# Layer 3 attention on one core: one product for q and k of a head, their parts doubled across the partitions by transfers

## What is computed

```
scale = Dh ** (-0.5)
q = (x @ Wq).reshape(B, N, H, Dh).transpose(0, 2, 1, 3)
kv = x @ Wkv
k = kv[..., :H * Dh].reshape(B, N, H, Dh).transpose(0, 2, 1, 3)
v = kv[..., H * Dh:].reshape(B, N, H, Dh).transpose(0, 2, 1, 3)
s = jnp.einsum('bhid,bhjd->bhij', q * scale, k)
gm = jax.lax.stop_gradient(jnp.max(s, axis=-1, keepdims=True))
causal_mask = jnp.triu(jnp.ones((N, N), bool), 1)
p = jnp.where(causal_mask, 0.0, jnp.exp(s - gm))
num = jnp.einsum('bhij,bhjd->bhid', p, v)
out = num / (jnp.sum(p, axis=-1, keepdims=True) + EPS)
```

## Time and profile before

| | |
|---|---|
| runs | 2026.16, 2018.31, 2021.64 us; median 2021.64 us |
| profiled execution | 2017.0 us, of it 2015.2 us from the first to the last instruction |
| busy share of that span | PE 85%, PEld 55%, DVE 71%, ACT 60%, POOL 55% |
| granted TensorE clock | 0.939 of full speed over the span |
| layer 3 attention | about 1008 to 2007 us, half of the span |

### The profile page before, as it was taken

One profiled execution on the slowest core, in us unless ns is written; L12 is line 12 of the kernel. 1 busy time (PEld: TensorE's weight loads), 2 busy tenths in 40 slices (PEclk: granted clock), 3 DMA queues, 4 the chain that ended last, 5 costly groups with the idle time before them and its releaser, 6 DMA issues. The chain is left out here.

```text
span 2015.2 us, 30793 instructions
## 1 busy us (share of the span) xinstructions
PE 1719.5 (85%) x10655; PEld 1111.6 (55%) x10655; DVE 1420.8 (71%) x2090; ACT 1200.7 (60%) x2046; POOL 1118.3 (55%) x1024
## 2 busy tenths in 40 slices
PE   6737999999577788877789999889999999989988
PEld 3414777788543377634634555555555555555564
DVE  3556777774254799854168888888888888888883
ACT  4374333326236577435358777777877777777860
POOL 1244554541400375212037888788888888888881
PEclk8667999998588999988989999999999999999999
DMA  2102222220100000004117999999889999999992
GB/s 70 35 30 76 79 85 69 84 80 26 32 6 14 13 1 1 1 11 125 43 27 136 159 159 159 163 160 162 160 154 157 159 163 166 160 159 162 164 164 58
DMA packets 632550, 193.08 MB, mean 96 GB/s; under 512 B 591601, under 2 KB 624130, under 8 KB 632398
## 3 DMA queue, kind: packets, MB, share of 16 engines
q1 hardware_dynamic: 624006, 167.56, 46.1%
q0 software_dynamic: 8224, 23.51, 3.9%
q10 hardware_dynamic: 168, 0.06, 0.0%
HBM read 36.90 MB, written 12.48 MB: 25 GB/s over the span
## 5 line engine op out<-in xcount | busy, mean ns | idle before, releaser
L2884 DVE TENSOR_REDUCE half_max<-scores 128x1 f32<-128x1024 f32 x512 | 614.8, 1219 | 131.9 <-PE scores L2666 126.3
L2583 POOL TENSOR_TENSOR p_low<-p,p_high 128x2048 f16<-128x2048 f32 (+15 forms) x256 | 576.3, 2251 | 150.7 <-ACT p_high L2810 126.0
L2666 PE MATMUL scores<-k_high,q_pair 128*128 128x512 f16 x1024 | 303.7, 378 | 66.0 <-ACT p L2795 61.1
L2795 ACT ACTIVATE p<-scores,exp_bias 128x1024 f32<-128x1024 f32 (+7 forms) x384 | 317.4, 861 | 68.5 <-DVE exp_bias L2889 66.3
L2810 ACT ACTIVATE p_high<-p 128x2048 f16<-128x2048 f32 (+15 forms) x256 | 282.6, 1104 | 40.6 <-DMA pT_high<-p_high 32.8
L2666 PE MATMUL scores<-k_low,q_pair 128*128 128x512 f16 x1024 | 304.2, 379 | 0.0
L2686 PEld LDWEIGHTS scores<-v_pair,pT_high 128*128 128x128 f16 x2176 | 149.8, 98 | 103.5 <-issue 61.4
L2686 PE MATMUL scores<-v_pair,pT_low 128*128 128x129 f16 x2176 | 183.9, 220 | 11.5 <-DMA pT_low<-p_low 11.2
L2686 PE MATMUL scores<-v_pair,pT_high 128*128 128x129 f16 x2176 | 186.4, 220 | 3.8 <-DMA pT_high<-p_high 3.6
L2686 PEld LDWEIGHTS scores<-v_pair,pT_low 128*128 128x128 f16 x2176 | 145.2, 98 | 46.7 <-DMA pT_low<-p_low 15.7
L2666 PEld LDWEIGHTS scores<-k_low,q_pair 128*128 128x128 f16 x1024 | 99.2, 97 | 121.7
(11 more groups left out here) (491 smaller groups left out, 3210.1 us busy)
## 6 DMA issues: line engine op xcount, KB each, us to landing
pT_high<-p_high SPq DMA_TRANSPOSE x256, 3.6
pT_low<-p_low SPq DMA_TRANSPOSE x256, 3.7
slots<-zero_row SPq DMA_DIRECT2D x1, 3036.0 KB, 14.1
slot_rows<-slots SPq DMA_DIRECT2D x23, 132.0 KB, 2.4
slots_out<-expert_out SPq DMA_DIRECT2D x23, 128.0 KB, 1.8
w_up<-in_L_ffn_inter_w_dram SPq DMA_DIRECT2D x1, 2048.0 KB, 8.8
x_tokens<-in_L_attn_x_dram SPq DMA_DIRECT2D x4, 256.0 KB, 3.5
dispatched<-moe_rows SPq DMA_DIRECT2D x1, 1024.0 KB, 10.3
```

The costliest lines, as they stand in the source:

```text
L2583: pool.tensor_tensor(flat(pl[:, buf, b0:b0 + n, :]), flat(p32[:, buf, b0:b0 + n, :]), flat(ph[:, buf, b0:b0 + n, :]), ALU.subtract).then_i ...
L2666: mm = pe.matmul(ps[:, b.start + i, :], q, k[:, par, cs(2 * half + i)], start=start, stop=not start)
L2795: act.activation(flat(p32[:, buf, b0 + first:b0 + first + w, :]), flat(ps[:, banks(p, half), :])[:, 0:w * P], ACT.Exp, bias=bias[:, p:p + ...
L2884: dve.tensor_reduce(mx[:, p % 2, half:half + 1], flat(ps[:, b[half], :]), AX.X, ALU.max, negate=True)\
```

## The change

q and k of a head come from one product: the tile `w_qk` holds the 64 columns of Wq and, beside them, the 64 columns of Wk of the head, so that partitions 0 to 63 of the result are q and 64 to 127 are k. A head has 4 units, not 8, in steps 0 to 3. ACT makes the high part of both with one operation, whose scale is a column (0.125 for q, 1.0 for k), DVE the low part of both. What the doubled weights did is done by eight transfers for each head, each of 64 partitions by 1024 16-bit numbers (128 KB): `move_k` writes k low and k high into the two halves of `k_pair`, and `move_q`, which waits for that, overwrites the k halves with q, so that one tile holds (q high; q low) and the other (q low; q high). SP issues them in positions 4 and 8 (`move_k`) and 6 and 10 (`move_q`), half of the tokens at a time. The loads of weights are two per head, not four, and stand in position 12, not 5. The scores take the two q tiles with the one k tile. In the prologue the moves of head 0 run one behind the other.

```diff
-                        for dst, src in ((wq, inp["L3_attn_Wq"]), (wk, inp["L3_attn_Wkv"])):
-                            for r in range(2):
-                                sp.dma_start(dst[:, h % 2, r, :], src[:, ds(h * DH, DH)]).then_inc((w_loaded0, w_loaded1)[h % 2], 16)
+                        for r, src in enumerate((inp["L3_attn_Wq"], inp["L3_attn_Wkv"])):
+                            sp.dma_start(wqk[:, h % 2, r, :], src[:, ds(h * DH, DH)]).then_inc((w_loaded0, w_loaded1)[h % 2], 16)
+                    def move_k(at, par, x):
+                        wait(sp, qk_low, at(NCH, 2 * x + 2, 1))
+                        sp.dma_start(klh[hi, par, half_of(x)], qhl[hi, par, half_of(x)]).then_inc(k_moved, 16)
+                        sp.dma_start(klh[lo, par, half_of(x)], qlh[hi, par, half_of(x)]).then_inc(k_moved, 16)
+                    def move_q(at, par, x):
+                        wait(sp, k_moved, at(64, 32 * x + 32, 1))
+                        sp.dma_start(qhl[hi, par, half_of(x)], qlh[lo, par, half_of(x)]).then_inc(q_moved, 16)
+                        sp.dma_start(qlh[hi, par, half_of(x)], qhl[lo, par, half_of(x)]).then_inc(q_moved, 16)
...
+                        for x in range(2):
+                            move_k(at, 0, x)
+                            move_q(at, 0, x)
...
-                            if p == 5 and not last and h + 2 < H:
-                                wait(sp, q_raw, at(NCH, NCH))
+                            if p in (4, 8) and not last:
+                                move_k(at, 1 - par, p // 4 - 1)
+                            if p in (6, 10) and not last:
+                                move_q(at, 1 - par, (p - 6) // 4)
+                            if p == 12 and not last and h + 2 < H:
+                                wait(sp, qk_raw, at(NCH, NCH))
                                 load(h + 2)
...
                         if p == 0 and half == 1:
-                            wait(pe, k_lows, now(NCH, NCH))
-                            wait(pe, q_low, now(NCH, 2))
-                        if p == NT // 2 and half == 1:
-                            wait(pe, q_low, now(NCH, NCH))
-                        q = qs2[:, par, ORDER[p] * P:(ORDER[p] + 1) * P]
-                        for k, start in ((kh2, True), (kl2, False)):
+                            wait(pe, q_moved, now(64, 64))
+                        for q, start in ((qhl, True), (qlh, False)):
                             for i in range(2):
-                                mm = pe.matmul(ps[:, b.start + i, :], q, k[:, par, cs(2 * half + i)], start=start, stop=not start)
+                                mm = pe.matmul(ps[:, b.start + i, :], q[:, par, ORDER[p] * P:(ORDER[p] + 1) * P],
+                                               klh[:, par, cs(2 * half + i)], start=start, stop=not start)
...
-                                    if (i, half) == (0, 0) and not last:
+                                    if (i, half) == (0, 0) and not last and s < NCH:
                                         unit_free(at, s)
                                         project(at, 1 - par, s, UBANK)
...
+                        act.activation(qhl[:, par, cs(u)], ps[:, b, :], ACT.Copy, scale=scales[:]).then_inc(qk_high, 1)
...
+                        dve.scalar_tensor_tensor(out=qlh[:, par, cs(u)], in0=ps[:, b, :], scalar=scales[:], in1=qhl[:, par, cs(u)],
+                                                 op0=ALU.mult, op1=ALU.subtract).then_inc(qk_low, 1)
```

More of the change, by code:

```diff
@@ L2465, in layer3_attention @@
             sb = lambda name, shape, dt=F32: inner.enter_context(nc.sbuf_tensor(f"{name}_{nc.next_id()}", shape, dt))
-            wq, wk, wv = sb("w_q2", [P, 2, 2, DH]), sb("w_k2", [P, 2, 2, DH]), sb("w_v", [P, H * DH])
+            wqk, wv = sb("w_qk", [P, 2, 2, DH]), sb("w_v", [P, H * DH])
+            scales = sb("qk_scales", [P, 1])
             v_all = o_all[:].bitcast(F16)
-            qs2, kh2, kl2 = (sb(n, [P, 2, TOK], F16) for n in ("q_pair", "k_high", "k_low"))
+            qhl, qlh, klh = (sb(n, [P, 2, TOK], F16) for n in ("high_then_q", "low_then_q", "k_pair"))
             v2 = sb("v_pair", [P, 2, NT, VW + 1], F16)
@@ L2635, in unit_free @@
                     def unit_free(at, u):
-                        kind = UNITS[u - 1][0]
-                        wait(pe, q_low if kind == "q" else k_lows, at(NCH, unit_count((u - 1) % PAIRS), 1 if u else 0))
+                        wait(pe, qk_low, at(NCH, u, 1))
                     def project(at, par, u, b):
-                        kind, c = UNITS[u]
                         if u == 0:
[L2644 to L2647, removed]
+                            wait(pe, (w_loaded0, w_loaded1)[par], at(16, 32 - 16 * par, 1))
+                        pe.matmul(ps[:, b, :], wqk[:, par, :, :].rearrange("p r d -> p (r d)"), m.xn[:, cs(u)],
+                                  start=True, stop=True).then_inc(qk_raw, 1)
                     def values(n, g, b):
@@ L2739, in prologue @@
                             values(u // 2, u % 2, u % 8)
-                        for u in range(len(UNITS)):
+                        for u in range(NCH):
                             pe.wait_ge(v_low, 2 * NT - 7 + u)
                             project(at, 0, u, u % 8)
-                        pe.wait_ge(q_low, NCH)
+                        pe.wait_ge(v_low, 2 * NT)
+                        pe.wait_ge(qk_low, NCH)
                         for p in range(2):
@@ L2773, in high @@
                     def high(at, par, u, b):
[L2775 to L2781, removed]
+                        wait(act, qk_raw, at(NCH, u + 1, 1))
+                        act.activation(qhl[:, par, cs(u)], ps[:, b, :], ACT.Copy, scale=scales[:]).then_inc(qk_high, 1)
                     def values_high(n, g, b):
@@ L2832, in head @@
                                     split(*shift(at, par, 2 * s + i - 1)[::2])
-                                if i and not last:
+                                if i and not last and s < NCH:
                                     high(at, 1 - par, s, UBANK)
@@ L2838, in prologue @@
                             values_high(u // 2, u % 2, u % 8)
-                        for u in range(len(UNITS)):
+                        act.wait_ge(scales_set, 2)
+                        for u in range(NCH):
                             high(at, 0, u, u % 8)
@@ L2859, in low @@
                     def low(at, par, u, b):
[L2861 to L2865, removed]
[L2866 to L2870 removed]
+                        wait(dve, qk_high, at(NCH, u + 1, 1))
+                        dve.scalar_tensor_tensor(out=qlh[:, par, cs(u)], in0=ps[:, b, :], scalar=scales[:], in1=qhl[:, par, cs(u)],
+                                                 op0=ALU.mult, op1=ALU.subtract).then_inc(qk_low, 1)
                     def values_low(n, g, b):
@@ L2917, in prologue @@
                     def prologue(at):
+                        dve.memset(scales[lo], SCALE).then_inc(scales_set, 1)
+                        dve.memset(scales[hi], 1.0).then_inc(scales_set, 1)
+                        dve.wait_ge(scales_set, 2)
                         for u in range(2 * NT):
                             values_low(u // 2, u % 2, u % 8)
-                        for u in range(len(UNITS)):
+                        for u in range(NCH):
                             low(at, 0, u, u % 8)
```

22 lines of the change are left out of this document (7 added, 15 removed).

## The result

The kernel after takes 2007.98 us (median of 8 runs, 2003.35 to 2016.48), the kernel before 2019.03 us (2014.86 to 2026.16): ratio 0.995, interval 0.9929 to 0.9971. The profiled execution has a span of 2006.1 us, 9.1 less than before.

What follows compares the result with a forecast made beforehand. The prediction took SP's issue queue as the bound, at 57.1 us a head. Moves and loads, +46.9 us, and the prologue, +3.6, made +50.5 on the median of 2021.64: 2072 us, range 2013 to 2098.

Steps and rivals of the forecast that it cites:

- The bound: SP's issue queue always has work waiting; a head takes 57.1 us because SP takes that long to issue it.
- The test that was set: Profile after: SP without gaps, its transposing transfers again 3 to 10 us behind their data.
- The other test: A head near 53 us in the profile after would prove the bound wrong; near 60.2 us was expected.
- the rival of the engines: DMA engines, not SP's issue, are the limit, with 4 us a head free: 2082 us and up, chance 0.08.
- the term of the 32 transposing issues: SP's transposing transfers per head: some 55 us of issues in the steady state, left unchanged in the sum.
- issue gives way: Rival: SP's transposing issues shrink to 46.4 us a head, PE and DVE decide: 1964 to 2010 us, chance 0.15.
- Moves and loads, +46.9: SP's queue: eight moves a head at 0.51 us add 61.2 us, two loads fewer a head take off 14.3.
- that branch: Main case, the queue of SP sets the pace: 2072 us, 2050 to 2090, chance 0.64.
- The units, priced at 0: Four units a head taken from PE, DVE and ACT: 0, up to 4.1 us a head if the bound is wrong.
- The new wait of PE, 2 us or more: Next head's first scores on PE wait for the last moves to land, 2 us or more, at no cost in time.
- This costs nothing as long as SP has work: PE's wait ahead of a head's first scores adds no time; the cover at position 0 is 3.4 us.
- The prologue, +3.6 and 0 for the clock: Ahead of head 0, moves delay the first scores 3.6 us; a granted clock of 0.50 costs 0 to 3, taken as 0.

Runs made afterwards that it cites:

- the kernel before with its tiles shifted: Kernel before with 32 unused bytes a partition ahead of p, so all five p and pT tiles begin at multiples of 256 bytes: 1982.27 us, ratio 0.9813.
- the shifted-back kernel: Kernel after with 224 unused bytes ahead of p, so the p and pT tiles stand 224 bytes past a multiple of 256 again: 2084.73 us, ratio 1.0319.
- the run with the second half earlier: Kernel after with the moves of the second half of tokens one SP position earlier, k at 7 and q at 9: 2012.39 us, ratio 0.9955.

## Why the prediction was wrong

**The bound was right as far as the runs can tell.** SP's queue was never without work before: gaps of over 0.2 us make 0.2 us a head, 0.9 in the kernel after, and 4.2 and 4.0 in the kernel before with its tiles shifted and in the run with no moves. The test that was set, transposing transfers 3 to 10 us behind their data, is met in the kernel after too (3.4 to 7.6 us for the high parts, in the mean of each position from 1 on), but it is a weak one. `turn_high` also waits for a free place (`summed`), and with no moves, where SP does wait, the high parts are 2.1 to 4.5 us behind as well. The other test, the head near 53 us that "would prove the bound wrong", was not met at 56.05.

What no run tells apart is whether SP's issues are long of themselves or because of the DMA engines behind them. The times of a head's 256-byte packets, added up and divided by 16 engines, are 51.7 us before, 45.9 with the tiles shifted and 50.0 with the moves from ACT; the transposing issues took 52.2, 46.4 and 50.3. So the rival of the engines is not excluded for the kernel before. Its price was wrong in the prediction all the same: it says that 4 us a head are free and then adds the 3.8 us of the moves in full.

**The step that failed** is the term of the 32 transposing issues, some 55 us a head with what lies between (52.2 without), which the sum left as it was. In the kernel after they are 46.4, since its tiles stand at multiples of 256 bytes: 5.8 us a head less. 46.4 is the figure of the rival *issue gives way*, with 51.5 together with moves and loads; measured were 52.5, and 56.0 with what lies between, which that rival left out. It had the size and not the cause, and that 2008 us lies within its 1964 to 2010 is luck. It let the issue give way when other things change, and the kernel before with 32 bytes more shows all of the 5.8 us with no unit gone; in the shifted-back kernel, where the units are gone and the place is bad, 1.7 of them are left (50.5 us, 2085 us in all). The cause stands in a line of the diff that I read as a constant, `scales`, and in what it does to all places behind it. I did not work out one address. Nothing in the trace of before says "misplaced". The issues of 1.58 us in head 0 and of 3.30, which I laid to the DMA engines, don't say it either: both read from badly placed rows, and the kernel after has one of 3.47 us, at 1531.86.

**Moves and loads, +46.9.** At the old place the change costs 67 us (2084.73 - 2017.55), inside the range of that branch (2050 to 2090). By the profiled spans of 2084.8 and 2015.2: 52.0 over the 13 heads, 11.9 ahead of them, 5.7 behind. The heads' term was mis-sized in the moves, 0.78 us each there and 0.64 in the kernel after, where I took 0.51 from the loads; at the old place the 1.7 us by which transposing issues became shorter hid a part of that.

**At the good place the same change costs 26 us**, since the engines' 54.81 us a head leave SP some idle time that the moves use first: 13 x (56.05 - 54.81) = 16.1, and 9.3 ahead of the heads. A price on a queue depends on whether the queue is the bound before the change.

**The units, priced at 0.** Right in kind. Even with SP out of the way they give 1.5 us a head of the 4.1.

**The new wait of PE, 2 us or more.** It came, 1.7 us a head, and brought stretches with the granted clock at 0.50, which the prediction priced at the start of head 0 alone. "This costs nothing as long as SP has work" is what the run with the second half earlier shows.

**The prologue, +3.6 and 0 for the clock.** Too small. The timelines of SP and of PE, and the windows, all of the kernel after:

```profile
1047.18 0.54 SPq L2522 DMA_DIRECT2D k_pair<-high_then_q  x1
...
1050.08 0.46 SPq L2528 DMA_DIRECT2D high_then_q<-low_then_q  x1
...
1054.18 0.46 SPq L2528 DMA_DIRECT2D high_then_q<-low_then_q  x1
1054.68 0.60 SPq L2529 DMA_DIRECT2D low_then_q<-high_then_q  x1
```
```profile
1043.76 3.60 PE L2658 MATMUL scores<-xn_features,w_qk 128*128 128x512 f32 x8
1057.11 1.01 PE L2674 MATMUL scores<-k_pair,high_then_q 128*128 128x512 f16 x2 [9.75 <-DMA low_then_q<-high_then_q]
```
```profile
1050.80:1054.20 3.40, 0.00 (x0) 0.00 (x0) 0.00 (x0) 0.66 (x1) 0.00 (x0) 0.50 0.67 154
1054.20:1057.60 3.40, 0.49 (x2) 0.25 (x3) 0.00 (x0) 0.00 (x0) 0.00 (x0) 0.50 0.33 77
1057.60:1061.00 3.40, 3.40 (x11) 1.24 (x10) 1.66 (x2) 0.00 (x0) 0.00 (x0) 0.61 0.00 0
```

The first scores start at 1057.11, 5.6 us later than in the earlier trace rows and not 3.6. PE was idle 9.75 us, and the granted clock stood at 0.50 (1.2 of 2.4 GHz) when the scores began: two of them took 1.01 us, before 0.60. This is the repeat of the earlier trace rows that I priced at 0 to 3 and set to 0. Of the 2.0 us that the term missed, 0.9 lie ahead of the first move (1047.18 against the 1046.29 of the forecast), 1.1 in the four rounds of issue and landing. By the first `den`, which is written in head 1, 8.9 us are lost: 0.6 ahead of the layer (its first product starts at 1013.17, before at 1012.53), 5.0 more up to the first scores, 3.3 behind them.

**Open.** Why a fifth of the badly placed packets take 20 to 60 ns while most keep the 18 ns of the well placed ones, and how SP's issue feels it, no run shows. Nor is it shown what makes transposing issues longer beside moves from another queue, or beside four large moves in place of eight.

## What to carry to other kernels

Work out the byte address of every tile that a transfer reads in short rows, before and after a change: a new 4-byte constant can move all tiles behind it, and its effect may be larger than that of the change. Before crediting a change with a gain, run the old code with the new places, and the new code with the old ones. And where a queue sets the pace, removing a wait elsewhere only moves it: sum the queue's issues over a period and compare that sum. Look, too, at whether the issues that stay become longer when others go: here they took back most of what fewer moves on SP had saved.

## What was not expected of the hardware

- A transposing transfer from one SBUF tile to another whose 256-byte rows begin at 128 or 224 past a multiple of 256 had packets of 23.2 and 23.4 ns in the mean, at 0 some 20 to 21 ns; SP's 32 issues a head took 52 against 46.4 us. Only the place of the source counted.
- Moves of 64 partitions x 2048 bytes took 0.64 us each to issue on SP (0.78 with the transposing reads badly placed), where loads of 32 KB took 0.5; the moves of q landed 2.6 to 2.7 us after issue in the median.
- A pair of such moves from ACT's queue, 1.1 us of issue, left ACT without work for 2.1 us in the mean, 3.3 at most.
- The transposing issues of a head on SP took about as long as the 16 DMA engines were busy with their packets, in three kernels: 52.2 and 51.7 us, 46.4 and 45.9, 50.3 and 50.0.
